# Two GpSimd folds moved ahead of the fifth expert's subtractions, and ScalarE's split of that expert moved behind the fifth activation

## The reference

```python
# L0_xattn: k = v = ctx, q = layernorm(x)
kv = jnp.einsum('bhil,bhjl->bijhl', k_, v_)
kv_f = jnp.fft.rfft(kv, n=fft_size)
y = jnp.fft.irfft(kv_f * kernel_f, n=fft_size)[..., :L]
out = y + kv * D[None, None, None, :, None]
out = jnp.einsum('bijhl,bhil->bjhl', out, q_)
...
# L0_ffn: x is the layernorm of the first result
router_probs = jax.nn.softmax(router_logits, axis=-1)
top_k_probs, top_k_indices = jax.lax.top_k(router_probs, K)
gates = jnp.einsum('bsk,bske->bse', top_k_probs, onehot)
expert_out = jax.nn.gelu(jnp.einsum('bsh,ehd->ebsd', x, expert_w) + expert_b[:, None, None, :])
combined = jnp.einsum('bse,ebsd->bsd', gates, expert_out)
return jnp.einsum('bsd,df->bsf', combined, out_w) + out_b
...
x = x + jnp.tanh(g_xattn[0]) * _L0_xattn_ref(ctx_2048, ctx_2048, _layernorm(x, axis=-1), ...)
x = x + jnp.tanh(g_ffn[0]) * _L0_ffn_ref(_layernorm(x, axis=-1), ...)
```

## Time and profile before

| what | value |
|---|---|
| median of 3 runs | 114.28 us (113.07 to 115.13) |
| the profiled execution, own time | 112.66 us |
| its span, first to last instruction | 110.9 us |
| mean granted clock of TensorE | 0.985 |
| PE busy | 103.0 us, 93% of the span |
| DVE busy | 90.0 us, 81% |
| POOL busy | 61.5 us, 55% |
| ACT busy | 57.6 us, 52% |

### The profile page before, as it was taken

One profiled execution on the slowest core, in us unless ns is written; L12 is line 12 of the kernel. 1 busy time (PEld: TensorE's weight loads), 2 busy tenths in 40 slices (PEclk: granted clock), 3 DMA queues, 4 the chain that ended last, 5 costly groups with the idle time before them and its releaser, 6 DMA issues.

```text
span 110.9 us, 1928 instructions
## 1 busy us (share of the span) xinstructions
PE 103.0 (93%) x578; PEld 87.8 (79%) x578; DVE 90.0 (81%) x297; ACT 57.6 (52%) x145; POOL 61.5 (55%) x81
## 2 busy tenths in 40 slices
PE   4939999999999999999699999999999999999970
PEld 4929988789989977867498888886787888888960
DVE  0186899999999999999999978688389986767860
ACT  4072668077236177664469797864464253452600
POOL 3024899999999959999999999900000000000000
PEclk9995899999999999999999999999999999999999
DMA  2967999268566540003000000000000111010022
GB/s 77 298 191 181 299 373 324 77 192 289 183 134 194 174 126 3 0 7 91 0 0 6 0 0 0 0 0 0 0 0 6 47 47 42 8 47 14 34 69 79
DMA packets 11092, 10.02 MB, mean 90 GB/s; under 512 B 1314, under 2 KB 11082, under 8 KB 11082
## 3 DMA queue, kind: packets, MB, share of 16 engines
q1 hardware_dynamic: 9570, 8.78, 27.1%
q10 hardware_dynamic: 1512, 1.12, 3.4%
HBM read 8.82 MB, written 1.07 MB: 89 GB/s over the span
## 4 chain that ended last, share of the span: by engine, by line
PE 51%; DVE 22%; POOL 12%; DMA 6%; issue 5%; ACT 1%; SPq 1%; DVEq 0%; POOLq 0%
PE ring L875 12%; PE ring L877 11%; PE ring L876 11%; DVE zq_t L1062 6%; POOL zq_t L419 5%; DVE zq_t L1064 5%; PE red L817 3%; DVE kv_t L387 3%; DMA ctx_t<-in_ctx 3%; DMA dcol<-in_L_xattn_D 3%; DVE zq_t L1066 2%; DVE zq_t L1067 2%; PE zbank L919 2%; POOL kv_t L387 2%; PE red L743 2%
## 5 line engine op out<-in xcount | busy, mean ns | idle before, releaser
L1164 DVE SCALAR_TENSOR_TENSOR mix_t<-ring,ctxT_t,mix_t 128x256 f32<-128x256 f32 x53 | 25.4, 483 | 6.1 <-ACT ring L631 4.4
L631 ACT ACTIVATE ring<-ring 128x512 f32<-128x512 f32 (+1 forms) x32 | 18.2, 567 | 18.4 <-PE ring L877 18.3
L387 POOL TENSOR_TENSOR kv_t<-ctxT_t 128x320 f32<-128x320 f32 x25 | 21.5, 888 | 7.8 <-ACT ctxT_t L543 5.9
L875 PE MATMUL ring<-w_hi_t,zT_hi_t 128*128 128x512 f32 (+1 forms) x64 | 25.6, 401 | 0.0
L877 PE MATMUL ring<-w_hi_t,zT_lo_t 128*128 128x512 f32 (+1 forms) x64 | 24.6, 385 | 0.0
L876 PE MATMUL ring<-w_lo_t,zT_hi_t 128*128 128x512 f32 (+1 forms) x64 | 24.5, 383 | 0.0
L793 PE MATMUL ring<-kv_t,toep_t 128*128 128x288 f32 x64 | 21.4, 416 | 0.0
L794 PEld LDWEIGHTS ring<-kv_t,toep_t 128*128 128x128 f32 x64 | 12.2, 190 | 3.4
L877 PEld LDWEIGHTS ring<-w_hi_t,zT_lo_t 128*128 128x128 f32 x64 | 12.0, 188 | 2.5
L875 PEld LDWEIGHTS ring<-w_hi_t,zT_hi_t 128*128 128x128 f32 x64 | 12.0, 188 | 2.4 <-DVE mix_t L1164 0.2
L876 PEld LDWEIGHTS ring<-w_lo_t,zT_hi_t 128*128 128x128 f32 x64 | 12.1, 189 | 1.9
(11 more groups left out here) (139 smaller groups left out, 177.2 us busy)
## 6 DMA issues: line engine op xcount, KB each, us to landing
ctx_t<-in_L_ffn_expert_w SPq DMA_DIRECT2D x8, 256.0 KB, 4.3
toep_t<-kpad_dram SPq DMA_DIRECT2D x3, 512.0 KB, 6.5
x_t<-in_x SPq DMA_DIRECT2D x8, 128.0 KB
out<-x_t SPq DMA_DIRECT2D x7, 128.0 KB
wlast_t<-in_L_ffn_expert_w SPq DMA_DIRECT2D x1, 768.0 KB, 6.2
ctx_t<-in_ctx ACTq DMA_DIRECT2D x2, 256.0 KB, 3.1
zq_t<-in_x ACTq DMA_DIRECT2D x2, 256.0 KB, 3.9
ctx_t<-in_ctx SPq DMA_DIRECT2D x2, 256.0 KB, 3.7
```

Of the source, the lines that this page charges most:

```text
L387: eng.tensor_tensor(dst, head.unsqueeze(1).to_broadcast([P, HB + 1, HD * CB]), windows(ctxT_t, g, h, HB + 1), ALU.mult).then_inc(done, 1)
L631: act.activation(y, y, ACT.Gelu_apprx_tanh).then_inc(gelu_ready, 1)
L875: pe.matmul(y, hi, whi, start=(c == 0), stop=False)
L1164: dve.scalar_tensor_tensor(out=acc, in0=block_bank(n)[:, L * e:L * (e + 1)], scalar=gate, in1=acc, op0=ALU.mult, op1=ALU.add).then_inc(mix ...
```

## The change

POOL's two folds go ahead of its subtractions for the fifth expert (e = 4). ACT's split of that expert, which waits for those subtractions, goes behind `activate(4)`. No instruction is added, removed or altered; no DMA is touched.

```diff
             relative(pool, 3, weights_relative)
-            relative(pool, 4, weights_relative)
             weights_low(pool, 3, weights_low_ready)
             fold(pool, 1, 0, pool_folded)
             fold(pool, 1, 2, pool_folded)
+            relative(pool, 4, weights_relative)
             relative(pool, 5, weights_relative)
...
             z_high(3)
-            split_weights(4)
             activate(0)
...
             activate(3)
             activate(4)
+            split_weights(4)
             split_weights(5)
             projection_high()
```

## The result

The changed kernel takes 114.85 us (median of 6 runs) against 113.51 us of the kernel before (6 runs), a ratio of **1.012, 95% interval 1.0073 to 1.0167**: about 1.4 us slower. One of the six executions took 133.78 us at a mean granted clock of 0.757; it has no profile, the ratio leaves it out, and its cause stays open. The profiled execution took 114.45 us, with a span of 111.9 us (before: 112.66 and 110.9).

What follows compares the result with a forecast made beforehand. PE, busy 93% of the span, was taken to bound the kernel. The 1.2 us lost at experts(5) added to the runs' median of 114.28 us gave 115.5 us, 1.1% slower; range 114.4 to 117.0 us.

Steps and rivals of the forecast that it cites:

- The turns: At the folds: order becomes POOL, DVE, POOL, DVE; all four done 0.63 us earlier, but DVE's last 1.61 us later.
- The size of the term: At experts(5): PE stands idle for its bank and starts at about 58.47 instead of 57.26, 1.2 us lost.
- What lies behind it: DVE's chain from choose_values(0) to accumulate(0) moves whole by 1.61 us; PE's loss at experts(5) isn't recovered later.
- second rival: At the folds: no blocking, or DVE does both in one turn; not slower, 114.2 us; chance 0.09.
- its own case: The forecast's case, 1.15 to 1.4 us lost at experts(5): 114.9 to 116.2 us; chance 0.66.
- third rival: At the folds: POOL still comes after DVE, its late list costs 0.5 us at z_transposed(7), 114.8 us; chance 0.08.
- PE's clock: Rival: after 1.6 us idle ahead of experts(5) the clock falls to half, losing 1.7 us more, 117.2 us; chance 0.17.
- Folds that don't block each other: One form of the not-slower rival: POOL's folds end 0.6 us earlier, DVE's at 53.1 or before; 114.2 us, shared chance 0.09.
- DVE doing both of its folds in one turn: Other form of the not-slower rival: DVE's folds end by 53.5 us, accumulate(0) frees the bank in time; shared chance 0.09.
- POOL coming second: Rival: POOL's first fold not there by 48.55, folds end as before, z_transposed(7) 0.5 us late, 114.8 us; chance 0.08.
- the 1.88 us of the prediction: PE's only long earlier idle time between matmuls, ending at 8.38 us, soon followed by half clock; used for the clock rival.

Runs made afterwards that it cites:

- the order alone: Kernel before, DVE's first fold also waiting for weights_low(3), so POOL is just ahead: ratio 1.016 (three of five times); run again for a second profile, 114.28 us.
- the kernel with POOL's lead: Kernel before, DVE's first fold waiting for weights_low(3) and behind an added 256-element copy from PSUM, so POOL's fold is 0.43 us ahead: ratio 1.0142.
- the two kernels with one engine's folds alone: Kernel before without DVE's two folds, and without POOL's two; PE adds six planes instead of four: 113.82 and 114.46 us, one run each.
- the run that forces it: Changed kernel, with POOL's first fold also waiting for z_low(3), so DVE's first fold is issued ahead of it: ratio 1.0072.
- the run with POOL's part alone: Kernel before with the folds ahead of relative(4), but ACT's split_weights(4) still ahead of activate(0): ratio 1.0766.
- the run of 119.5 us: Profiled execution of the kernel before with DVE's first fold also waiting for weights_low(3); 119.5 us, left out of that kernel's ratio 1.016.

## Why the prediction was right

**The turns: right.** The order POOL, DVE, POOL, DVE came as forecast, with POOL's first fold 0.18 us ahead of z_low(3) (forecast 0.19). The two executions of the order alone in which the turns held have PE waiting 1.49 and 1.50 us ahead of `experts(5)` without any of the change's edits, and the kernel with POOL's lead makes 1.014.

**The size of the term: right, and a little low.** The forecast had 1.2 us at `experts(5)`; it was 1.39. Nearly all of the missing 0.19 us lies in the folds: DVE's last one ended 6.65 us after z_low(3), not 6.48. I had taken 2.25 us for each fold of POOL, worked out from instructions that were already waiting when DVE's ended. The first one starts with no fold of DVE's under way, and such a fold takes 2.41 us (2.42 with POOL's folds alone).

**What lies behind it: right.** The chain to `accumulate(0)` moved as a whole (forecast end 10.20 us after z_low(3), measured 10.37), the 0.45 us of slack was used up, and the loss went through to the end (1.39 at `experts(5)`, 1.43 at the last products).

**A step that was wrong and cost nothing.** The prediction let `relative(4)` run from 53.60 us, right behind POOL's last fold, and so had `relative(5)` 0.3 us early. By its own rule `relative(4)` has to wait for DVE's last fold, and it did: `relative(5)` starts 7.89 us after z_low(3) (55.77) instead of 7.07 (55.29), 0.82 us late. PE is 1.4 us late by then and doesn't wait for it. The prediction's second rival had these 0.8 us; its forecast did not.

**The level of the median.** The forecast of 115.5 us was built on the 114.28 us of the three runs shown, 1.62 us above the profiled execution. With six runs the median before is 113.51, and the measured 114.85 lies where the ratio puts it: 1.011 forecast, 1.012 measured. As a time by itself it lies 0.05 us under the 114.9 to 116.2 that the prediction gave to its own case, and next to the 114.8 of the third rival. So the time alone doesn't pick the case; the order of the folds and the wait ahead of `experts(5)` do.

**The rivals.** PE's clock did not fall after 1.50 us of idle time; three other runs with a gap of 1.49 or 1.50 us ahead of `experts(5)` kept a granted clock of 1.00 in the 8 us around and behind it. The prediction had no row between 0.87 and 1.88 us, so that the clock would stay was a chance it had priced and not a thing it had worked out. With 6.87 us the clock fell. Folds that don't block each other are refuted by the two kernels with one engine's folds alone, and DVE doing both of its folds in one turn by the ends in the changed kernel (51.20 and 54.53, POOL's 53.45 between). POOL coming second was not what happened; the run that forces it lost 0.64 us where the prediction gave 0.5, though from `z_transposed(5)` on and not at `z_transposed(7)` alone.

The Trainium skill, page "SBUF — State Buffer", section "Who interferes with whom", says that issue order decides who blocks. The trace agrees for the first turn of every profile here: 1.21 us for DVE's first fold when it came first, 2.99 when POOL was there 0.51 us earlier.

## What to carry to other kernels

A duration in a row can hold another engine's work: when equal instructions on VectorE and GpSimd take 1.2 and 3.4 us, write their ends one under the other before pricing anything. Where two engines take turns, starting one of them earlier shortens the whole by little (0.46 us here) and can change who is last, so ask which engine's last instruction has the longer chain behind it and let that one go first. And a late list that costs nothing behind a longer wait shows its price as soon as that wait is taken away: the two have to be mended together.

## What had not been expected

- Taking turns is not certain. In one execution of the order-alone kernel a fold of DVE, issued 0.07 us behind POOL's, stood for 9.71 us behind seven POOL instructions; in another execution of the same kernel, with the same 0.07 us, it had its turn after one (3.42 us). In the nine other profiles here in which both engines had their folds to do, nobody was passed over. What decides it wasn't found.
- A fold of POOL takes 2.38 to 2.43 us when no fold of DVE's is under way, but its part of a turn, from the other's end to its own, is 2.25 us. The 0.15 us can be start-up done while waiting; that was only argued.
- The length of PE's idle time doesn't settle whether TensorE's granted clock falls. It fell after 1.88 us at the start of the kernel before, within 6.87 us in the run with POOL's part alone and within the 5.16 us ahead of the sums in the run of 119.5 us. It stayed at 1.00 through 1.50 us ahead of `experts(5)` in the changed kernel, but also through 2.79 us at the start of that same execution, and through 2.75 us at the start of the second profile of the order alone. So the 1.88 us of the prediction is no measure for another gap; what decides it stays open here.
